# ScalarE's order in two binarised convolution layers: the neighbours' transfers and the sign of a chunk ahead of the high halves of new pieces

## The reference, cut to what matters

```python
x = x + _L0_conv_ref(_gn(x), ...)   # weights binarised, own weights at every position
x = x + _L1_conv_ref(_gn(x), L1_conv_weights)
x = x + _L2_conv_ref(_gn(x), ...)   # as the first
x = x + _L3_conv_ref(_gn(x), ...)   # all products of pairs in a row, mixed by weights

# inside the first and the third layer
def binarize(x):
    scale = jnp.mean(jnp.abs(x))
    return jnp.sign(x) * scale
wb = binarize(weight)[0]
out = jnp.einsum('bchwk,ochwk->bohw', patches, wb)   # 3 x 3 patches
```

## Time and profile before

| what | value |
|---|---|
| median of 3 runs | 730.81 us (726.95 to 737.42) |
| profiled execution, its own time | 727.99 us |
| its span | 726.2 us |
| busy: PE, DVE, ACT, POOL | 497.3, 570.6, 432.4, 415.6 us |
| loop of the first layer | about 39 to 141 us of the span |
| loop of the third layer | about 323 to 425 us of the span |

### The profile page before, as it was taken

One profiled execution on the slowest core, in us unless ns is written; L12 is line 12 of the kernel. 1 busy time (PEld: TensorE's weight loads), 2 busy tenths in 40 slices (PEclk: granted clock), 3 DMA queues, 4 the chain that ended last, 5 costly groups with the idle time before them and its releaser, 6 DMA issues.

```text
span 726.2 us, 53531 instructions
## 1 busy us (share of the span) xinstructions
PE 497.3 (68%) x24392; PEld 386.4 (53%) x24392; DVE 570.6 (79%) x730; ACT 432.4 (60%) x738; POOL 415.6 (57%) x653
## 2 busy tenths in 40 slices
PE   4537575409479999806666623626898898898988
PEld 4536565409368888605566621204565565565665
DVE  4699999898833534489999989955788787797877
ACT  5359999574011212227999948314677676676765
POOL 3389885004435651029888201546878878878762
PEclk9867979957799999965988975967899999999999
DMA  8939999600169999956999930015899999999995
GB/s 344 422 134 393 396 397 396 256 0 1 22 248 377 394 394 397 413 221 235 391 400 401 375 136 0 1 27 165 296 330 373 389 330 406 336 339 408 324 414 236
DMA packets 48100, 209.10 MB, mean 288 GB/s; under 512 B 8241, under 2 KB 15409, under 8 KB 35761
## 3 DMA queue, kind: packets, MB, share of 16 engines
q1 hardware_dynamic: 38592, 201.67, 73.1%
q10 hardware_dynamic: 9216, 6.30, 2.9%
q0 software_dynamic: 240, 0.53, 0.2%
HBM read 193.79 MB, written 4.19 MB: 273 GB/s over the span
## 4 chain that ended last, share of the span: by engine, by line
PE 38%; DVE 19%; POOL 15%; issue 9%; DMA 9%; ACT 7%; ACTq 2%; SPq 0%; POOLq 0%; DVEq 0%
PE psum L921 15%; PE psum L1034 7%; PE psum L1008 6%; PE psum L945 5%; POOL xn_ring L283 5%; DMA beyond<-state_b 3%; DMA beyond<-state_a 3%; ACT state_b L659 2%; DVE xn_ring L283 2%; ACT signs L529 2%; PE psum L1020 2%; DVE state_a L826 2%; POOL near L402 2%; POOL state_b L488 2%; DVE state_b L881 2%
## 5 line engine op out<-in xcount | busy, mean ns | idle before, releaser
L881 DVE TENSOR_TENSOR state_b<-psum,state_b 128x512 f32<-128x512 f32 x256 | 169.3, 686 | 53.0 <-ACT state_b L659 47.4
L921 PE MATMUL psum<-signs,near 64*32 64x96 f16 (+3 forms) x6528 | 124.0, 216 | 100.8 <-DMA beyond<-nothing 37.8
L659 ACT ACTIVATE state_b<-psum 128x512 f32<-128x512 f32 x256 | 143.3, 595 | 72.7 <-PE psum L1008 70.0
L921 PEld LDWEIGHTS psum<-signs,near 64*32 64x32 f16 (+1 forms) x6528 | 111.5, 103 | 109.4 <-issue 109.0
L766 DVE TENSOR_REDUCE abs_sums<-wring 128x1 f32<-128x2048 f32 x64 | 142.9, 2277 | 0.1
L529 ACT ACTIVATE signs<-wring 128x2304 f16<-128x2304 f32 x64 | 135.0, 2110 | 0.0
L1034 PE MATMUL psum<-state_b,wring 128*32 128x32 f32 x8192 | 106.9, 202 | 9.2 <-issue 5.4
L1008 PE MATMUL psum<-signs,sel 64*128 64x512 f16 x516 | 89.9, 404 | 29.5 <-POOL signs L447 13.9
L1034 PEld LDWEIGHTS psum<-state_b,wring 128*32 128x32 f32 x8192 | 88.5, 114 | 40.3 <-issue 30.2
L921 PE MATMUL psum<-wring,near 64*32 64x96 f32 (+5 forms) x3264 | 96.8, 242 | 13.9 <-DMA beyond<-nothing 10.6
L447 POOL COPY signs<-wring 64x512 f16<-64x512 f16 x130 | 80.6, 620 | 33.6 <-PE psum L1008 27.4
(11 more groups left out here) (153 smaller groups left out, 880.3 us busy)
## 6 DMA issues: line engine op xcount, KB each, us to landing
wring<-in_w SPq DMA_DIRECT2D x96, 1152.0 KB, 11.1
wring<-in_pairs SPq DMA_DIRECT2D x64, 640.0 KB, 9.4
wring<-in_pairs SPq DMA_DIRECT2D x64, 512.0 KB, 8.5
state_a<-in_x SPq DMA_DIRECT2D x8, 512.0 KB, 9.4
beyond<-state_b ACTq DMA_DIRECT2D x112, 32.0 KB, 6.3
wring<-signs SPq DMA_DIRECT2D x56, 64.0 KB, 4.5
out<-state_a SPq DMA_DIRECT2D x7, 512.0 KB, 10.6
beyond<-state_a ACTq DMA_DIRECT2D x56, 32.0 KB, 5.9
```

The source lines that it names most:

```text
L659: act.activation(left[:, n % LSLOTS, :], psum[:, n % ASLOTS, :], ACT.Copy, scale=1.0 / HALF_SCALE / HALF_SCALE).then_inc(left_made, 1)
L881: dve.tensor_tensor(feats[:, n % FSLOTS, :], psum[:, ASLOTS + n % BSLOTS, :], left[:, n % LSLOTS, :], ALU.mult).then_inc(feats_made, 1)
L921: last = pe.matmul(psum[g * B:(g + 1) * B, bank, (a * C) % 512:(a * C) % 512 + (b - a) * C], acts[q, j, s, k, :], weights[q, j, kind, s, ( ...
```

## The change: what it does

In ScalarE's loop of the first and the third layer, b(n) and sign(n) now stand ahead of the high halves of chunk n. Chunk 0 keeps its order (its four high halves, then b(0)). Nothing is added or removed, on no engine; SyncE's, GpSimd's, VectorE's and TensorE's instructions keep their order.

```diff
                 for n in range(CHUNKS):
                     upto = min(CHUNKS, needed(n) + 3)
+                    used(layer, n)
+                    if n:
+                        load_beyond(layer, n)
+                    if n >= 2:
+                        sign_of(layer, n)
                     for e in range(ready, upto):
                         high_half(layer, e)
                     ready = max(ready, upto)
-                    used(layer, n)
-                    load_beyond(layer, n)
-                    if n >= 2:
-                        sign_of(layer, n)
+                    if n == 0:
+                        load_beyond(layer, n)
                     if n > PIECES and n % PIECES in (1, 2):
                         square_half(layer, 2 * (n // PIECES - 1) + n % PIECES - 1)
```

## The result

| | before | changed |
|---|---|---|
| median, runs | 732.28 us, 6 runs (726.95 to 737.42) | 744.94 us, 6 runs (740.37 to 746.88) |
| profiled execution, span | 727.99, 726.2 us | 741.80, 740.0 us |

A forecast was written before the change was run, and what follows sets the result against it. ScalarE was taken as full in both loops, so idle time at their heads delays their ends: 5.5 + 5.3 = 10.8 us on 727.99 gives 738.8, or 741.6 from the median; stated 740, range 729 to 747.

The forecast's parts named there:

- The sum: Delays of ScalarE's loops, 5.5 us in the first layer and 5.3 in the third, together 10.8 us slower.
- The chain: Chunks 2 to 4: sign, high half, GpSimd's low half, transfers, next sign run one after another, leaving ScalarE idle.
- sign(3): ScalarE's sign of chunk 3: 7.58 us behind the sign before it, adding 2.9 us in first layer, 2.6 in third.
- sign(4): ScalarE's sign of chunk 4: 4.90 us behind the sign before it instead of 2.73, adding 2.2 us in each layer.
- sign(2): ScalarE's sign of chunk 2: waits for chunk 1's later transfers, adding 0.4 us in first layer, 0.5 in third.
- b(5) and on: Transfers from chunk 5 on: issued by the time the sign under way ends, so no further idle time on ScalarE.
- rival A: Loop chunks without a square: longer transfers and low halves idle ScalarE again, 4 to 10 us more, 743 to 750; chance 0.17.
- the delay neither grows nor shrinks: ScalarE behind the first layer's loop head: full again and 5.5 us late, with no further loss per chunk.
- waits more for convolutions: costs nothing beyond ScalarE's delay: VectorE in the loops: starts its chunks where it did, its longer waits for convolutions adding nothing to ScalarE's delay.
- B: Rival: transfers leave without waiting for xn, VectorE's 5.0 us of convolution waits vanish, 723 or 726 us; chance 0.07.
- C: Rival: VectorE sets the loop's end and ScalarE's late start is taken up, no change, 728 to 731; chance 0.11.
- D: Rival: signs start while their transfers are being issued, two pairs of 1.26 per layer drop out, 734 to 737; chance 0.05.

The follow-up runs named there:

- e4: Changed kernel with GpSimd's low(7) moved ahead of near(2) and xn(8), ScalarE's order untouched; ratio 1.0083 to the kernel before.
- e8: Changed kernel with sign(n) ahead of the transfers b(n) for chunks 2 to 4, high halves still behind both; ratio 1.0010 to the kernel before.
- e1: Old order (high halves ahead) for chunks 0 to 3 of both loops, new order from chunk 4 on; ratio 0.9999 to the kernel before.
- e6: Kernel before with only chunk 3 of both loops in the new order, hi(8) and hi(9) behind its sign; ratio 1.0084 to the kernel before.
- e7: Kernel before, but at chunk 3 only hi(8) ahead of transfers and sign, hi(9) behind, new order from chunk 4; ratio 0.9981 to the kernel before.
- e3: New order in the first layer's loop only, old order in the third's; ratio 1.0063 to the kernel before.
- e9: Kernel before with chunk 3 as b(3), hi(8), sign, hi(9), new order from chunk 4, GpSimd's low(7) ahead of near(2) and xn(8); ratio 0.9962.

## Why the prediction was right

**Forecast and size.** 740 with a range of 729 to 747; measured 744.94. The sum was 10.8 us, measured 12.7 (10.0 to 15.4). No rival happened as a whole. The range of 729 to 747 is wide enough to take in the kernel before (732.28), so that 744.94 lies in it says little; and 740 was 1.6 below the sum's own 741.6, for which no reason was given. What supports the prediction is its steps.

**The chain.** It is shown, not argued: e4 shortened one of its links by 2.07 and the sign behind it came 2.05 earlier; e8 cut the link that the sign is queued behind its transfers, and the loss went away with the high halves still behind both; e1 put the high halves of chunks 1 to 3 back, and it went away too. sign(3) and sign(4) came with 2.90 and 2.19 more in the first layer, where 2.9 and 2.2 were worked out, in the third 2.59 and 2.19 for 2.6 and 2.2. sign(2) came with 0.27 and 0.50 for 0.4 and 0.5.

**A row misread, without effect on the sum.** The 0.85 us ahead of sign(3) in the earlier trace rows were taken as a wait for a low half, as the profile names it. b(3) needs low(7), which ran from 47.27 to 47.94. GpSimd's and ScalarE's timelines of the kernel before:

```profile
47.27 0.67 POOL L391 TENSOR_TENSOR state_b<-xn_ring,state_b 128x256 f16<-128x256 f32 x1
49.46 0.42 ACT L536 ACTIVATE state_b<-xn_ring 128x256 f16<-128x256 f32 x1 [0.55 <-POOL xn_ring L283]
49.47 0.51 ACTq L545 DMA_DIRECT2D beyond<-state_b  x1
```

The pair left at 49.47 only, because hi(9) stood in front of it and waited for xn(9). ScalarE's 0.85 us, from 49.88 to 50.73, are the time in which the pair was issued. Likewise the waits of the changed kernel came under "issue" instead of a low half, 4.41 and 1.79 us where 3 to 4 and 1.5 to 2 were expected.

**b(5) and on: small, not zero.** I had the pair of b(5) issued just when sign(4) ends. It held the sequencer for 1.40 (60.86 above) instead of 1.16, so sign(5) stood 2.91 behind sign(4) instead of 2.72, in the third layer 3.17 instead of 2.71. That is 0.2 and 0.5, rival A's mechanism in one chunk. Later chunks stayed at 2.72 and 3.33, as before, but for one: sign(26) stands 3.34 behind sign(25) instead of 3.02, in the third layer 3.33 instead of 3.03. Between sign(4) and sign(31) the new list has 22 high halves, hi(10) to hi(31), and the old one 21. That is 0.3 us per loop, which the sum put at nothing ("the delay neither grows nor shrinks"). Rival A as a loss in each chunk is refuted by e1, which has the new order in all chunks from 4 on.

**VectorE "waits more for convolutions: costs nothing beyond ScalarE's delay"** was the step with a fault, though not one that turned the result. The evacuation behind conv(3) waits 5.21 us, so VectorE's own nearly full list is late by about as much as ScalarE's. At the end of the first loop the changed kernel shows this:

```profile
145.02 0.71 DVE L761 STREAM_TRANSPOSE state_b<-psum 128x512 f32<-128x512 f32 x1
145.76 0.69 DVE L763 TENSOR_REDUCE row_sums<-state_b 128x16 f32<-128x512 f32 x1
146.37 0.70 DVE L761 STREAM_TRANSPOSE state_b<-psum 128x512 f32<-128x512 f32 x1
```

The last evacuation follows the one before it without a wait, where it waited 1.24 us for conv(31) before the change: there VectorE's list set the end. In the third loop it was the transfers again:

```profile
429.67 6.02 DMA beyond<-state_a
435.69 0.34 issue
436.03 2.25 PE psum L924 x121
...
438.30 0.73 DVE state_a L761
```

This piece of the chain of waits has b(31) landing in 6.02 and conv(31) in 2.25, where the third loop before had 5.53 and 1.63: 1.1 us on top of ScalarE's delay, the largest part that the sum did not have. The third loop adds up: 5.28 at sign(4), 0.46 at sign(5), 0.30 at sign(26) and 1.11 at the end are its 7.15. 5.5 and 5.3 were forecast, 5.95 and 7.15 came.

**Rivals.** B (b leaves earlier, faster): b(3) left at 16.8 us behind hi(0) instead of 13.6, the other way round. To issue early bought nothing here, because the transfer's own input was moved behind a sign. C (VectorE takes it up): refuted, both lists were late. D (the sign passes the transfers): L528 starts at 54.53, 0.10 after the second transfer of b(3) is issued; behind b(4) and b(5) it is 0.10 likewise. A sign in front of the transfers runs during their wait (e8). The sequencer rule of the Trainium skill ("Advanced Engine Details and Errata", Sequencer Loop), that other engine instructions can be read and queued while a control instruction executes, is not borne out by this trace for a sign behind these transfers.

## What to carry to other kernels

When an instruction moves behind a long one on its engine, look not at what now starts earlier but at who makes the input of the next thing in that list: a 0.4 us rounding moved behind a 2.1 us sign cost 2.9 us, because by way of GpSimd's low half it fed the transfers that the next sign is queued behind. Write such a chain out with start-to-start times of rows, once around; it gave sign(3) and sign(4) here to 0.1 us. Where it missed (e6, e7), a transfer held the sequencer 0.8 to 1.0 us longer than the row that was used for it. An engine that is full has no slack to take up a delay at its head, so the head of a loop, before it fills, is where an order is worth working out.

## What the runs showed of the hardware that was not expected

- A transfer of the same size and form held ScalarE's sequencer for 0.61 us in most rows, but 1.40 (e7), 1.80 (e1, third layer), and a pair 1.73 (e4) or 1.40 (changed kernel) instead of 1.16. These lie in chunks 3 to 5, near the time when the ring of weights begins to be loaded again (48.67 in the kernel before), but not all do: 0.85 at b(2) in the kernel before, ahead of that time, and 1.34 at 92.70 in e3. What they wait for wasn't tried.
- The neighbours' transfers took 5.7 to 6.6 us to land beside the weights, 6.1 in the median (kernel before, 60 to 136 us), and 1.8 us at the least in the head of the loop.
- TensorE stops once in the middle of conv(3) with nothing that the profile shows: 3.54 us in e9, 0.22 in e7, 1.56 in e6, and 4.24 in the third layer of e9. In each case one packet of 16 KB of an instruction queue starts 2.3 to 2.5 us before TensorE goes on (55.04 and 57.32, 53.80 and 56.08, 54.02 and 56.53, 341.01 and 343.38). That TensorE waits there for its own program fits these times; no run tried it. Where conv(3) begins later than that, as in the kernel before, the stop doesn't show.
